# Pacing 244 row gathers: from one wait per gather to bursts that wait for a step of TensorE and for a landing

## What is computed

```python
e = jnp.stack([tbl_0[ids[:, 0]], ..., tbl_25[ids[:, 25]]], axis=1)
T = jnp.concatenate([r_dense[:, None, :], e], axis=1)        # 2048 x 27 x 128
Z = jnp.einsum('bnd,bmd->bnm', T, T)
h = jnp.concatenate([Z[:, iu0, iu1], r_dense], axis=1)       # 351 pairs + 128
h = jnp.maximum(h @ W_top1 + b_top1, 0.0)                    # 479 -> 512
h = jnp.maximum(h @ W_top2 + b_top2, 0.0)                    # 512 -> 256
y = h @ W_top3                                               # 256 -> 1
```

## Time and profile before

| | us |
|---|---|
| runs, median | 453.94 |
| runs, lowest and highest | 452.58, 459.67 |
| the profiled execution, its own time | 448.83 |
| span of that execution in the profile | 447.0 |
| TensorE busy | 388.3 (87% of the span) |
| VectorE, ScalarE, GpSimd busy | 262.2, 156.7, 235.8 |

### The profile page before, as it was taken

The page is one execution under the profiler, slowest core; times in us unless marked ns, Lnnn a source line. Parts: engine busy times, 40 slices in busy tenths (PEclk is TensorE's granted clock), DMA queues, the critical chain, the costliest instruction groups (busy, mean ns, idle before and its releaser), DMA issues.

```text
span 447.0 us, 9767 instructions
## 1 busy us (share of the span) xinstructions
PE 388.3 (87%) x4139; PEld 353.5 (79%) x4139; DVE 262.2 (59%) x440; ACT 156.7 (35%) x215; POOL 235.8 (53%) x252
## 2 busy tenths in 40 slices
PE   7678487798988999889997999889997999898997
PEld 5568487687868889779887989779886889787897
DVE  4369558677736764666846674586845674572131
ACT  5236424251441615215351414325251424315321
POOL 6658555545655546645565456555565546556000
PEclk9869978998999999989999899999999999899899
DMA  8974211345231521234121531235121431242230
GB/s 210 252 213 125 56 47 45 96 99 166 55 85 41 140 73 41 72 90 125 37 85 42 121 92 41 84 70 148 39 67 48 105 109 48 54 108 75 41 52 18
DMA packets 48393, 39.26 MB, mean 88 GB/s; under 512 B 33073, under 2 KB 42592, under 8 KB 48350
## 3 DMA queue, kind: packets, MB, share of 16 engines
q1 hardware_dynamic: 38913, 22.38, 19.4%
q0 software_dynamic: 7808, 16.01, 14.1%
q10 hardware_dynamic: 1628, 0.25, 0.4%
HBM read 32.59 MB, written 6.03 MB: 86 GB/s over the span
## 4 chain that ended last, share of the span: by engine, by line
PE 78%; issue 10%; DVE 5%; another core or an unknown queue 3%; ACT 3%; DVEq 0%; ACTq 0%
PE look_ps L896 34%; PE gram_ps L928 15%; PE mlp_ps L948 9%; PE look_ps L906 6%; PE mlp_ps L958 5%; DVE hot L574 4%; PE look_ps L887 3%; ACT T L752 1%; ACT T L744 1%; PE look_ps L1000 1%; ACT tab_hi L719 1%; PE look_ps L970 1%; PE look_ps L992 1%; DVE hot L579 1%
## 5 line engine op out<-in xcount | busy, mean ns | idle before, releaser
L536 POOL DMA_INDIRECT rows<-in_tbl_dram,ids_all x228 | 219.2, 961 | 168.7 <-PE look_ps L896 58.3
L574 DVE TENSOR_TENSOR hot<-ids_near,gram_ps 125x2048 fp32r<-125x2048 f16 x60 | 135.7, 2285 | 77.0 <-PE look_ps L896 68.5
L896 PE MATMUL look_ps<-hot,tab_hi 125*128 125x256 f32 x664 | 172.2, 297 | 9.3 <-issue 4.2
L896 PE MATMUL look_ps<-hot,tab_lo 125*128 125x256 f32 x664 | 166.8, 289 | 0.0
L896 PEld LDWEIGHTS look_ps<-hot,tab_hi 125*128 125x128 f32 x664 | 131.5, 198 | 13.6 <-issue 7.5
L896 PEld LDWEIGHTS look_ps<-hot,tab_lo 125*128 125x128 f32 x664 | 131.7, 198 | 0.1
L744 ACT COPY T<-look_ps 128x512 f32<-128x512 f32 x38 | 45.4, 1196 | 205.2 <-PE look_ps L896 76.9
L928 PE MATMUL gram_ps<-T 128*54 128x54 f32 x2048 | 78.0, 222 | 37.3 <-issue 29.6
L928 PEld LDWEIGHTS gram_ps<-T 128*54 128x54 f32 x2048 | 66.3, 136 | 50.9 <-issue 43.0
L752 ACT COPY T<-look_ps 128x384 f32<-128x384 f32 (+2 forms) x80 | 75.7, 1050 | 34.3 <-PE look_ps L906 19.8
L606 DVE COPY gram<-gram_ps 128x486 f32<-128x486 f32 (+1 forms) x64 | 37.9, 606 | 40.4 <-remote 30.0
(11 more groups left out here) (81 smaller groups left out, 162.6 us busy)
## 6 DMA issues: line engine op xcount, KB each, us to landing
dots<-gram SPq DMA_DIRECT2D x28, 182.2 KB
ids_near<-ids_rows SPq DMA_DIRECT2D x25, 192.0 KB
rows<-in_tbl_dram,ids_all POOLq DMA_INDIRECT x228
T<-in_tbl_dram SPq DMA_DIRECT2D x4, 448.0 KB
pairs<-dots SPq DMA_DIRECT2D x14, 117.0 KB
gram<-in_tbl_dram SPq DMA_DIRECT2D x3, 448.0 KB
rows<-in_r_dense_dram SPq DMA_DIRECT2D x16, 64.0 KB
w<-in_tbl_dram SPq DMA_DIRECT2D x2, 448.0 KB
```

The costliest lines, as they stand in the source:

```text
L536: pool.indirect_dma_start(rows[:, t % 2, place[n], :], None, tables[n - 1], bass.IndirectOffsetOnAxis(ap=index[:, n - 1:n].bitcast(U32), a ...
L574: eq = nc.vector.tensor_tensor(hot[:VP, count % 2], near, steps[:VP].rearrange("p (c q) -> p c q", q=1).to_broadcast([VP, CH, Q]), ALU.is_ ...
L896: mm = pe.matmul(dst, w[:VP, k, c], hot[:VP, slot, c], start=(c == 0 and half == 0), stop=(c == CH - 1 and half == 1))
```

## The change

`STEP_MORE`, `STEP_LESS` and the old `keep_pace` go. The gathers are cut into bursts. Only the first gather of a burst waits: for the landing of the gather just before it (`wait_landed`), then for one step. The rest of a burst runs without a pacing wait; the `turned` waits at the first gather of a round stay. In units of 30 gathers the bursts begin at gathers 0, 7, 13, 16, 21 and 27 (so they have 7, 6, 3, 5, 6 and 3 gathers) and wait for steps 5, 11, 16, 20, 24 and 27 of `progress`. The last unit has a list of its own (`BURSTS_END`), and so have tiles 0 to 3 (`EARLY`).

```diff
-            STEP_MORE = (4, 5, 6, 6, 8, 8, 8, 10, 10, 11, 12, 12, 13, 13, 15, 16, 16, 17, 18, 19, 20, 21, 21, 22, 23, 23, 24, 25, 26, 26, 27, 28)
-            STEP_LESS = (4, 5, 6, 6, 8, 8, 8, 10, 10, 11, 12, 12, 13, 15, 16, 16, 17, 18, 19, 20, 21, 21, 22, 23, 24, 25, 26, 27, 28, 29)
+
+            EARLY = ({7: (hot_looked, 1), 12: (hot_looked, 3)},
+                     {0: (hot_looked, 5), 5: (hot_looked, 6), 10: (hot_looked, 9)},
+                     {0: (gram_done, 1), 6: (turned, 8), 11: (hot_looked, 14)},
+                     {0: (gram_done, 5), 6: (hot_looked, 17), 11: (turned, 15)})
+
+            BURSTS = {0: 5, 7: 11, 13: 16, 16: 20, 21: 24, 27: 27}
+            BURSTS_END = {0: 5, 7: 11, 13: 15, 16: 16, 21: 19, 27: 21}
...
+            def wait_landed(t, i):
+
+                v, at = (t, i - 1) if i else (t - 1, len([n for r in rounds_of((t - 1) // 2) for n in r if n]) - 1)
+                gathered = [(r, j) for r in range(NR) for j, n in enumerate(m for m in rounds_of(v // 2)[r] if m)]
+                r, j = gathered[at]
+                pool.wait_ge(rows_landed[v % 2][r], (rows_count(v // 2 - 1, r) if v >= 2 else 0) + 16 * (j + 1))
+
             def keep_pace(t, i):
 
-                if t == 0:
-                    if i == 14:
-                        pool.wait_ge(hot_looked, 2)
...
-                elif i not in (0, 3, 7, 11, 14 if t // 2 < ADDED else 13):
-                    u = t // 2 - 1
+                if t < len(EARLY):
+                    if i in EARLY[t]:
+                        wait_landed(t, i)
+                        pool.wait_ge(*EARLY[t][i])
+                    return
+                u, at = t // 2 - 1, 15 * (t % 2) + i
+                bursts = BURSTS if u + 1 < END else BURSTS_END
+                if at in bursts:
+                    wait_landed(t, i)
                     steps_u = progress(u) + (progress(u + 1) if u + 1 < END else [])
-                    pool.wait_ge(*steps_u[min((STEP_MORE[16 * (t % 2) + i] if u + 1 < ADDED else STEP_LESS[15 * (t % 2) + i]),
-                                          len(steps_u) - 1)])
+                    pool.wait_ge(*steps_u[bursts[at]])
```

More of the change, by code:

```diff
@@ L494, in progress @@
                         (turned, NR * (t + 2) + 3), (turned, NR * (t + 2) + 5)]
-            def keep_pace(t, i):
-                if t == 0:
-                    if i == 14:
-                        pool.wait_ge(hot_looked, 2)
[L501 to L513, removed]
-                elif i not in (0, 3, 7, 11, 14 if t // 2 < ADDED else 13):
-                    u = t // 2 - 1
+            def wait_landed(t, i):
[3 more added lines that the diff above has]
+                pool.wait_ge(rows_landed[v % 2][r], (rows_count(v // 2 - 1, r) if v >= 2 else 0) + 16 * (j + 1))
+            def keep_pace(t, i):
+                if t < len(EARLY):
[7 more added lines that the diff above has]
+                    wait_landed(t, i)
                     steps_u = progress(u) + (progress(u + 1) if u + 1 < END else [])
-                    pool.wait_ge(*steps_u[min((STEP_MORE[16 * (t % 2) + i] if u + 1 < ADDED else STEP_LESS[15 * (t % 2) + i]),
-                                          len(steps_u) - 1)])
+                    pool.wait_ge(*steps_u[bursts[at]])
             def gather(t):
```

## The result

| | before | changed |
|---|---|---|
| runs, median us | 453.94 | 483.47 |
| runs, lowest and highest | 452.58, 459.67 | 477.80, 484.86 |
| span of the profiled execution | 447.0 | 481.6 |
| granted TensorE clock, mean | 0.950 | 0.911 |

The ratio is 1.064, 95% interval 1.044 to 1.083. The forecast was 442.4 us with a range of 434 to 456.

What follows compares the result with a forecast made beforehand. TensorE, busy 87% of the span, was taken as the bound, with gathers starting inside product stretches holding it up. From 448.8 us, 9.5 (five units at 1.9) and 2.0 (start) gave 437.3, as a median 442.4 us, range 434 to 456.

Steps and rivals of the forecast that it cites:

- B: Second product stretch of a unit, 72 matmuls, 3.63 us, 1.67 lost; forecast to keep two gather starts and gain nothing.
- D: Fourth product stretch of a unit, 72 matmuls, 4.23 us; forecast to have no gather start left and gain 2.27 us.
- 6.6 us for 6 gathers, 1.1 us each: Price per gather starting inside a product stretch, from one unit's losses in three stretches with two gather starts each.
- A: First product stretch of a unit, 56 matmuls, 1.67 us, free; forecast to lose 1.1 to 2.2 us, 1.7 taken.
- C: Third product stretch of a unit, 56 matmuls, 4.17 us, 2.64 lost; forecast one gather start instead of two, gaining 1.3 us.
- a second trace: Looks' semaphores seen late by GpSimd, at 280.50 instead of near 278.2; given no separate term in the steady part.
- theory P: Follow-up theory: a gather starting inside a product stretch or in the last microsecond before it costs TensorE about 1.2 us.
- GpSimd falls behind: Rival, chance 0.04: with landings over 3.1 us bursts drift and transposes wait; 460 us at a landing of 3.5.
- The start: First tiles: seven gathers start by 10.6 us, the eighth waits for the look; gain 2 us, bounds 0 and 7.
- No change: Rival, chance 0.20: the losses belong to the products, so the time stays at 453.9 us, range 451 to 455.
- The losses move, slower: Rival, chance 0.11: gathers cost most after several in a row; A, B and C lose more, 458 to 477 us.
- the third step: Step to be judged by the first product stretch of a unit: over 3.5 us there would make it wrong.

Runs made afterwards that it cites:

- kernel of long bursts: Changed kernel with tiles 0 to 3 paced as before, bursts of 14, 3, 10 and 3 gathers behind product stretches, no landing waits: 503.65 us, ratio 1.119.
- plain copies: Kernel before, with tiles 4 to 15 starting a plain copy of a table's first 128 rows instead of each gather: 403.87 us, ratio 0.885.
- spaced kernel: Kernel before with no pacing from tile 4 on but a short memset, waited for, ahead of each gather: 559.74 us, ratio 1.233.

## Why the prediction was wrong

**What bounds the kernel.** Right in kind: the pauses inside the product matmuls are tied to the gathers. With the gathers replaced, on another chip of the slower kind, they are gone from the units concerned, and the kernel takes 404 us instead of 456.

**"Stretches with no gather start lose nothing."** Right for these stretches (B and D take 1.94 us), wrong as a guide to the time. The kernel of long bursts has hardly a gather in its product stretches and loses more elsewhere.

**"6.6 us for 6 gathers, 1.1 us each."** This is the step that failed, and with it "in A one inside and one at its edge, 1.7 taken". A lost 3.7. The price was put on the place of a gather; it is the run that counts. A now stands at the end of eleven gathers (five, 2.79 us idle, six). The trace before held the hint: the free A stood behind runs of two, and C, which lost most, at the end of twelve (seven, 1.82 us idle, five). I read the free A as "no gather starts inside" and divided the rest evenly by six. The place isn't nothing either: B lost 1.7 behind two pairs, of which the second starts inside it.

**"C has one instead of two."** C kept two gathers that start inside it, and a third (304.62) that still ran when it began. The burst of step 11 was laid at 278.4, the middle of the look, though the earlier trace rows show GpSimd acting on that same step only at 280.50. After the change the burst starts 1.5 us behind the middle of its look (299.35, burst at 300.87), on a 374-chip 0.8 us (182.28, 183.05). The semaphore's own events in the two traces, at 300.08 and 182.29, divide this up: the signal is 0.7 us late on the first and not at all on the second, and from the signal to the burst it is 0.8 us on both, where I had taken 0.3. The first gather of a burst has several waits, and one of them is an instruction of its own. I had noted the lag as "a second trace" and not used it where it mattered: with the burst at 280.5 its last gather starts at 286.8, and three start inside C (284.01 to 288.18), not one. C lost 1.0 more instead of 1.3 less.

**"B has two as before: nothing."** B has none and takes 1.6 us less. That is luck: the slow A and its look pushed B back from under its gathers.

**The clock.** Nothing in the sum. Longer pauses in A and C were followed by the lower clock, 2.5 us a unit; over the trace it is the largest term, 14.5 us. It was to be seen before: from 244.9 to 248.3, behind a D that had lost 2.3 us, the granted clock was 0.50. (So theory P's "over 3 us" is no bound of it either.)

**The landing.** I took 2.3 us, and named 3.1 as the limit beyond which GpSimd falls behind. The wait at 272.37 took 3.74 from gather to gather instead of 2.6: the last landing event that the trace holds for the gather at 268.63 is at 271.62, 3.0 us on, and the rest is the start behind two waits. It did little harm here, where a unit lasts 54 us, and it decides on a 374-chip, where the unit is 43.6 and landing waits alone cost 45 us. That rival had a chance of 0.04; on a faster chip it is the main one.

**The start.** Forecast a gain of 2 us, measured a loss of some 4. The first part was right beyond its bound: VectorE's idle stretch of 7.71 us is gone, and TensorE did its looks at 20 to 34 us, 10 us earlier than before. But the gathers that were held back then came late: the transposes of tile 0 waited for rows for 4.39 us up to 41.02. "Where before too gathers ran without pause" was the cover that didn't hold.

**Cover of the moved gathers.** Held in units 2 to 6 of the changed kernel: the transposes wait for no rows there. Ahead of the first A of unit 1 they waited 4.06 us, still from the start.

**The rivals.** "No change", and the rule of the Trainium skill behind it (SBUF — State Buffer, "Who interferes with whom", by which TensorE never waits for another engine, and so not for the gathers), is refuted on the 449-chips by the plain copies (456 us against 404), and the 374-chips agree with it (a product stretch of 1.61 us under gathers). "The losses move, slower" was the nearest: it had A and C at the end of runs losing more, and the reason given ("a gather may cost most when several have gone before it in a row") is what the runs showed. Its time, 471 to 477, lacked the clock. It was nearest in part by luck: it let B lose more and D keep its loss, and both came out free. It got 0.11, though the trace before had the longest run of gathers ahead of its costliest stretch. The unit on the changed trace: A +3.7, look +1.5, B -1.6, C +1.0, look +1.1, D -2.2, wait ahead of A +0.7, together 4.2 us.

**Slips in the working that moved nothing.** 20 of 30 gathers had a pacing wait before, not 24 (each of five rounds per tile excepts its first). A landing of 3.5 us makes 52.8 us of a unit's gathers, not 52.2 (24 x 1.25 + 6 x 3.8), and "GpSimd falls behind" then comes to 464 us, not 460. Of the signs named beforehand, D at 2.0 us without a pause came true, and A over 3.5 us, the one that was to make the third step wrong, came true with 5.3.

## What to carry to other kernels

A price worked out from "what stood beside a slow stretch" needs a case in which the neighbour stands elsewhere; without one, move the work a little and take the price of the whole run, not of the place. When a burst is assembled out of paced work, look for what its companions had been doing in the idle times between. And before one explains a difference, run the unchanged kernel beside it: here the same program takes 374 or 450 us by the chip, and on one kind the landing waits cost, on the other the bursts.

## What the runs showed of the hardware

- The same kernel takes 374 us on some chips and 449 to 456 on others. With gathers replaced in tiles 4 to 15 the slower kind comes down to 404, and its units to 43.6 us, the length they have on the faster kind. What sets the chips apart, no run tells; in the traces they can be told by the share of the gathers' semaphore events that is on record (98% against 29 to 42%).
- On the slower kind, matmuls go on for some 40 to 80 of their number from a run's first gather to the first pause of over 0.2 us in a row of matmuls: 43 in B and 57 in C of the kernel before, 56 to 61 in the changed kernel's C, 57 to 65 in the spaced kernel's long runs, 79 to 82 in the runs of 14. Then they come one to four per gather. That instructions are what is missing is inferred: the pauses have no semaphore that ends them and hit every kind of matmul, but the transfers of instructions that the traces show go on as on the faster kind. No single size of the store fits all cases.
- A signal that TensorE raised while gathers ran reached GpSimd 0.7 to 2.1 us late on the slower kind (looks with their middles at 299.35 and 278.15), and ScalarE and VectorE 4 us late behind ten gathers in a row. On the faster kind the one looked at was on time (182.28, 182.29).
- A gather's landing took 2.4 to 4.1 us on a 374-chip (54 gathers of the changed units there; the median is 2.6), not 2.3. While the DMA engines were full at the start it was about 7.8 us (the changed kernel, from 10.54 to the gather at 18.58 that waited for it).
- Pauses of 2.3 to 2.6 us inside a product stretch were followed by the lower clock (0.57 granted over the 4 us behind A); over the span the lower clock cost 14.5 us outside the product stretches.

None of the kernels that still gather all rows beat the one before on either kind of chip. The bursts without landing waits equal it on a 374-chip (1.004) and lose 7.3% on a 449-chip; so the old pacing, with its short runs, stays.
